# Attention's queries and row maxima laid out by DMA instead of by matrix products, its visits moved in the slot table, and a gap of three slots instead of four

## The reference, cut to what matters

```python
x = x + attn_a(layernorm(x))   # 32 heads of 4, two decaying recurrent states per head
x = x + ffn(layernorm(x))      # 8 experts of width 512, every token through all of them
x = x + attn_b(layernorm(x))   # causal softmax attention, 16 heads of 8, one shared key and value
x = x + ffn(layernorm(x))      # the same FFN weights again
```

```python
q = (x @ Wq + bq).reshape(B, T, 16, 8); k = (x @ Wk + bk)[:, :, None, :]; v = (x @ Wv + bv)[:, :, None, :]
q = rope(q); k = rope(k)
att = einsum('bthd,bThd->bhtT', q, k) / sqrt(8)
att = softmax(where(causal, -inf, att))
out = einsum('bhtT,bThd->bthd', att, v).reshape(B, T, 128) @ Wo + bo
```

## Time and profile before

| | us |
|---|---|
| runs of the kernel before | 1619.76, 1625.97, 1626.56 (median 1625.97) |
| the profiled execution | 1626.03 |
| its span | 1624.0 |
| PE busy | 1496.0 (92%) |
| DVE, ACT, POOL busy | 1177.7, 885.3, 784.3 |
| FFN tiles 9 to 13, from first gate to next first gate | 101.2 each |
| FFN tile 14 | 91.0 |
| FFN tile 15, with no attention beside it | 74.6 |
| granted clock | 1.00 from 855.0 on, but for the last us |

### The profile page before, as it was taken

The page is one execution under the profiler, slowest core; times in us unless marked ns, Lnnn a source line. Parts: engine busy times, 40 slices in busy tenths (PEclk is TensorE's granted clock), DMA queues, the critical chain, the costliest instruction groups (busy, mean ns, idle before and its releaser), DMA issues. The chain is left out here.

```text
span 1624.0 us, 23328 instructions
## 1 busy us (share of the span) xinstructions
PE 1496.0 (92%) x7504; PEld 1111.4 (68%) x7504; DVE 1177.7 (73%) x1949; ACT 885.3 (55%) x1520; POOL 784.3 (48%) x732
## 2 busy tenths in 40 slices
PE   3478999899989899899999999999999999999998
PEld 2356777677776677577567676776767767677786
DVE  5678787869778787868677585775857758577565
ACT  2245556464554546444655557565575655755554
POOL 2537445543525244531315546555465554655565
PEclk8689999999999999999999999999999999999999
DMA  6125543434334343433332334333343333433352
GB/s 202 59 71 179 198 154 119 156 117 156 140 133 156 117 156 117 156 117 117 117 133 101 118 117 150 123 131 117 119 156 121 125 117 122 156 119 124 148 182 112
DMA packets 36380, 216.28 MB, mean 133 GB/s; under 512 B 3491, under 2 KB 17444, under 8 KB 19876
## 3 DMA queue, kind: packets, MB, share of 16 engines
q1 hardware_dynamic: 36260, 214.79, 36.5%
HBM read 200.10 MB, written 15.27 MB: 133 GB/s over the span
## 5 line engine op out<-in xcount | busy, mean ns | idle before, releaser
L531 POOL TENSOR_TENSOR HL<-HF,HH 128x512 fp32r<-128x512 f32 x312 | 416.0, 1333 | 476.4 <-ACT HH L705 475.3
L1215 DVE TENSOR_TENSOR HF<-SG,bank 128x512 f32<-128x512 f32 x512 | 350.4, 684 | 171.8 <-PE bank L874 92.1
L872 PE MATMUL bank<-XTH,W 128*128 128x512 f32 x1024 | 423.4, 413 | 10.4 <-ACT SG L698 9.9
L874 PE MATMUL bank<-XTH,W 128*128 128x512 f32 x1024 | 403.8, 394 | 0.0
L873 PE MATMUL bank<-XTL,W 128*128 128x512 f32 x1024 | 403.6, 394 | 0.0
L1198 DVE SCALAR_TENSOR_TENSOR SG<-SG,bank 128x512 f32<-128x512 f32 x288 | 197.3, 685 | 207.0 <-ACT SG L700 205.0
L700 ACT ACTIVATE SG<-bank 128x512 f32<-128x512 f32 x288 | 172.1, 597 | 318.0 <-PE bank L874 316.5
L705 ACT ACTIVATE HH<-HF 128x512 fp32r<-128x512 f32 x512 | 320.4, 626 | 37.6 <-DVE HF L1215 32.4
L698 ACT ACTIVATE SG<-bank 128x512 f32<-128x512 f32 x224 | 133.5, 596 | 251.7 <-PE bank L874 250.4
L872 PEld LDWEIGHTS bank<-XTH,W 128*128 128x128 f32 x1024 | 194.4, 190 | 82.3 <-issue 23.6
L872 PE MATMUL dbank<-HH,W 128*128 128x512 f32 x512 | 217.9, 426 | 16.1 <-DVE HL L1204 14.9
(11 more groups left out here) (212 smaller groups left out, 1796.7 us busy)
## 6 DMA issues: line engine op xcount, KB each, us to landing
W<-kept_w SPq DMA_DIRECT2D x120, 1536.0 KB, 6.3
kept_w<-W SPq DMA_DIRECT2D x8, 1536.0 KB, 6.2
X<-in_L_attn_a_x_dram SPq DMA_DIRECT2D x8, 256.0 KB, 5.7
WS<-in_L_ffn_Wg_dram SPq DMA_DIRECT2D x8, 256.0 KB, 6.4
WS<-in_L_ffn_Wu_dram SPq DMA_DIRECT2D x8, 256.0 KB, 6.7
WS<-in_L_ffn_Wd_dram SPq DMA_DIRECT2D x8, 256.0 KB, 6.5
out_dram<-X SPq DMA_DIRECT2D x8, 256.0 KB, 7.2
CST<-in_tables_dram SPq DMA_DIRECT2D x1, 834.0 KB, 6.4
```

The source lines that it names most:

```text
L531: g.tensor_tensor(HL[:, n % HRING, :], HF[:, n % HFRING, :], HH[:, n % HRING, :].bitcast(F32), ALU.subtract).then_inc(F.hl, 1)
L872: pe.matmul(dst, wh, xh, start=start, stop=False)
L874: return pe.matmul(dst, wl, xh, start=False, stop=stop)
L1215: v.tensor_tensor(HF[:, n % HFRING, :], gated, fbank[(2 * n + 1) % 3], ALU.mult).then_inc(F.mul, 1)
```

## The change

Six things change together.

1. The queries' layout QST is made by DMA. SP writes QKH and QKL to DRAM (`kept_q`) and reads them back into QST, twelve reads of 8 partitions x 4 x 512 per tile. `query_stack` and its four cells are gone, with ACT's four copies. SP waits for the low part QKL and writes it before it issues the reads of the high part.
2. The maxima are transposed once per sequence (cell `mx`, `turn_maxima`, 64 columns), copied by ACT to MT, written to DRAM (`kept_m`) and read back into two free rows of each group of QST. Q2, NMP, SELR and the four `stack` cells are gone. `cols` reads QST directly, with 26 rows, and `rows` with 24.
3. The `cols` cells stand in neighbouring slots, all at point 2. PT holds six pieces in a ring instead of four, and the exponential stands ahead of ACT's gate activation instead of behind it.
4. `GAP` is 3 instead of 4, `B_LEAD` 35 instead of 36. For tile 0 the start stays the same slot.
5. The input's `turn` moves from relative slot -19 to -17, the projections from -8 to -11, and what ends the tile is one slot earlier (`fturn` 32 instead of 33).
6. SP walks the slots too, so its list now has the attention's DMAs between the weight loads.

```diff
-GAP = 4
+GAP = 3
-B_LEAD = 36
+B_LEAD = 35
-B_CELL = {"turn": (-19, 1, 3), "q": (-8, 2, 0), "qs": (-7, 1, 1), "k": (-7, 2, 2), "ks": (-6, 1, 0), "v": (-5, 1, 1),
-          "qst0": (-3, 2, 0), "qst1": (-2, 1, 1), "qst2": (-2, 2, 2), "qst3": (-1, 1, 0),
...
+B_CELL = {"turn": (-17, 1, 3), "q": (-11, 2, 0), "qs": (-10, 1, 1), "k": (-10, 2, 2), "ks": (-9, 1, 0),
+          "v": (-8, 1, 1), ("mx", 0): (8, 1, 3), ("mx", 1): (14, 1, 3), ("pv", 0, 0): (17, 1, 3),
...
-COLS_AT = [[(12, 2), (14, 0), (15, 2), (17, 0)], [(18, 2), (20, 0), (21, 2), (23, 0)]]
+COLS_AT = [[(12, 2), (13, 2), (14, 2), (15, 2)], [(17, 2), (18, 2), (19, 2), (20, 2)]]
+PT_RING = 6
...
+            def spread_queries(t, part, src, done):
+                for g in range(NG):
+                    to = RG * g + DB * part
+                    rows = kept_q[src, RG * g:RG * (g + 1), :].rearrange("(j x) t -> x j t", j=NJ)
+                    sp.dma_start(QST[to:to + DB, :, :].bitcast(F32), rows).then_inc(done, 16)
+
+            def spread_maxima(n, b):
+                sp.wait_ge(B.mt_out, 32 * (n + 1))
+                rows = kept_m[b].rearrange("(r g j) t -> g r j t", r=2, g=NG)
+                for g in range(NG):
+                    to = RG * g + 3 * DB
+                    sp.dma_start(QST[to:to + 2, :, b * SEQ:(b + 1) * SEQ].bitcast(F32),
+                                 rows[g]).then_inc(B.mrow, 16)
+
+            def side_b(t, r):
+                if r == -8:
+                    sp.wait_ge(B.hi, 2 * t + 1)
+                    after(sp, B.st_hi, 8 * 16 * t)
+                    sp.dma_start(kept_q[0], QKH[:, 0, :].bitcast(F32)).then_inc(B.hi_out, 16)
+                if r == -7:
+                    sp.wait_ge(B.lo, 2 * t + 1)
+                    after(sp, B.st_lo, 4 * 16 * t)
+                    sp.dma_start(kept_q[1], QKL[:, 0, :].bitcast(F32)).then_inc(B.lo_out, 16)
+                    sp.wait_ge(B.hi_out, 16 * (t + 1))
+                    after(sp, B.t_ready, 8 * t)
+                    spread_queries(t, 0, 0, B.st_hi)
+                    spread_queries(t, 1, 0, B.st_hi)
+                if r == -6:
+                    sp.wait_ge(B.lo_out, 16 * (t + 1))
+                    spread_queries(t, 2, 1, B.st_lo)
+                for b in range(SPT):
+                    n = SPT * t + b
+                    if r == B_CELL["mx", b][0]:
+                        sp.wait_ge(B.mt, n + 1)
...
+                            sp.dma_start(kept_m[b, :, a * P:(a + 1) * P],
+                                         MT[32 * a:32 * (a + 1), b, :].bitcast(F32)).then_inc(B.mt_out, 16)
+                    if r == B_CELL["mx", b][0] + 1:
+                        spread_maxima(n, b)
+
+            for slot in range(0, G_LAST + 1):
+                for t, r in b_tiles(slot):
+                    side_b(t, r)
+                for x in range(NE, 2 * NT * NE):
+                    u = FC * (x - WRING + 1) - 1
+                    if slot == ffn_slot(u // UNIT) + u % UNIT + LAG + 1:
+                        load_weights(x)
...
-                if n is not None:
-                    gate_act(n)
                 for t, r in b_tiles(slot):
                     for b in range(SPT):
                         for i, (at, point) in enumerate(COLS_AT[b]):
-                            if r == at + (point == 2):
+                            if r == at + 1:
                                 exps(SPT * t + b, i)
+                if n is not None:
+                    gate_act(n)
...
-            def stack2(n, b, h, bk):
-
-                pe.wait_ge(B.nml, 2 * (n + 1))
-                for x in range(2):
-                    j = 2 * h + x
-                    dst = bk[:, x * SEQ:(x + 1) * SEQ]
-                    pe.matmul(dst, SELR[:, SID, :], QST[:, j, b * SEQ:(b + 1) * SEQ], start=True, stop=False)
-                    for a in range(2):
-                        m = pe.matmul(dst[:, a * P:(a + 1) * P], NMP[:, b, a, j, :], SELR[:, SID, :],
-                                      start=False, stop=(a == 1))
-                m.then_inc(B.q2_ready, 1)
+            def turn_maxima(n, b, bk):
+
+                pe.wait_ge(B.nml, n + 1)
+                pe.transpose(bk[0:64, 0:P], NMS[:, b, :].bitcast(F32), ident).then_inc(B.mx, 1)
```

More of the change, by code:

```diff
@@ L334, in program @@
         KST = take("KST", TOK, dt=F32R)
[L335 to L339, removed]
+        assert at["now"] <= r_at
+        PT = take("PT", 3 * PT_RING, TOK)
         OS = take("OS", 2, TOK)
@@ L355, in program @@
                       "rs ay y xb z zsum zg zb done")
[L356 to L357 removed]
+        B = sems("b", "proj roped u_q u_k hi lo v_ready v_used hi_out lo_out st_hi st_lo kst_used row_ready row_used nmh nml "
+                      "mx mt mt_out mrow t_ready t_used t_cut pv os turn ro o ot otc out biased done")
         F = sems("f", "gate up sil half mul hh hl hlv down ys back done")
@@ L497, in _, with load_weights @@
             sp.dma_start(BRAW[:, C:], row(b_bk)).then_inc(ld.wb, 16)
-            for x in range(NE, 2 * NT * NE):
+            def load_weights(x):
                 sp.wait_ge(F.down, FC * (x - WRING + 1))
@@ new lines, in spread_maxima @@
+            def spread_maxima(n, b):
[25 more added lines that the diff above has]
+                        sp.wait_ge(B.mt, n + 1)
+                        after(sp, B.mrow, 4 * 16 * (n - 1))
+                        for a in range(2):
+                            sp.dma_start(kept_m[b, :, a * P:(a + 1) * P],
+                                         MT[32 * a:32 * (a + 1), b, :].bitcast(F32)).then_inc(B.mt_out, 16)
+                    if r == B_CELL["mx", b][0] + 1:
+                        spread_maxima(n, b)
@@ new lines, in _ @@
+            for slot in range(0, G_LAST + 1):
[5 more added lines that the diff above has]
+                        load_weights(x)
+                        if x % NE == 4 and x // NE > NT:
+                            t = x // NE - NT - 1
+                            sp.wait_ge(F.done, NT + t + 1)
+                            sp.dma_start(o_tok[:, t], X[:, t, :, :]).then_inc(stored, 16)
@@ L775, in exps @@
             def exps(n, i):
+                m = (4 * n + i) % PT_RING
                 act.wait_ge(B.t_ready, 4 * n + i + 1)
-                after(act, B.pv, 2 * n)
-                act.activation(PT[:, 3 * i:3 * i + 3, :], three, ACT.Exp, scale=DB ** -0.5).then_inc(B.t_used, 1)
+                after(act, B.pv, 2 * (n - 1) if i < 2 else 2 * n)
+                act.activation(PT[:, 3 * m:3 * m + 3, :], three, ACT.Exp, scale=DB ** -0.5).then_inc(B.t_used, 1)
             def side_b(t, r):
@@ L810, in side_b @@
                             act.activation(OS[:, z, :], abank, ACT.Copy).then_inc(B.os, 1)
-                    for h in range(2):
-                        if r == B_CELL["stack", b, h][0]:
-                            act.wait_ge(B.q2_ready, 2 * n + h + 1)
-                            after(act, B.t_ready, 4 * (n - 1))
-                            act.activation(Q2[:, b, 2 * h:2 * h + 2, :], r3(sbank[bank_of(("b", t, ("stack", b, h)))], 2),
-                                           ACT.Copy).then_inc(B.q2_used, 1)
+                    if r == B_CELL["mx", b][0]:
+                        act.wait_ge(B.mx, n + 1)
+                        after(act, B.mt_out, 32 * (n - 1))
+                        act.activation(MT[0:64, b, :], sbank[bank_of(("b", t, ("mx", b)))][0:64, 0:P],
+                                       ACT.Copy).then_inc(B.mt, 1)
                     if r == B_CELL["ot", b][0]:
@@ L840, in _ @@
                 n = unit_of(slot)
-                if n is not None:
-                    gate_act(n)
+                if slot == b_slot(0):
+                    act.wait_ge(A.done, NT)
+                    act.wait_ge(A.z, NT)
                 for t, r in b_tiles(slot):
@@ L1482, in _ @@
                 n = unit_of(slot)
+                if slot == b_slot(0):
+                    v.wait_ge(A.z, NT)
+                    v.wait_ge(A.done, NT)
                 new_maxima(slot, 2)
```

153 lines of the change are left out of this document (58 added, 95 removed), and 2 rows, old and new, of the table B_CELL.

## The result

The changed kernel takes **1674.06 us** (median of 3 runs, 1673.77 to 1674.5), the kernel before 1625.97. The ratio is 1.031, 95% interval 1.027 to 1.035: slower by 48 us, where 1614 and a range of 1589 to 1634 were forecast.

The account below looks back on a forecast made before the run. PE, busy 92% of the span, was taken as the bound. FFN tiles 8 to 13 -1.5 us, tile 7 -4.4, tile 14 -1.9, tile 6 -1.1, gap -3: together -11.9 from 1626.0, so 1614, range 1589 to 1634.

Parts of the forecast that it names:

- lands at 7.8 + 6.3 = 14.1: Slot 23's weight load, issued 7.8 us into it, lands 6.3 later; PE waits 2.7 us at slot 28.
- the reads pile up: Rival, 0.08: twelve reads at half a weight load's rate delay the load behind by 1 us in six tiles; 1620.
- SyncE's issues: Behind the wait for QKL, thirteen DMAs at 0.47 us each, 6.1 us, precede slot 23's weight load.
- issues are slow: Rival, 0.09: SP takes 0.85 us a read issue, not 0.47; wait at slot 28 is 7.6 us; 1649.
- The clock: After PE's pause at slot 28, half clock for 3.4 us loses 1.7; half counted, 0.85 us a tile.
- PE's savings and the small terms: Each full tile: PE saves 4.8 us net; ACT costs 0.3, layer norm 0.2, the wait for maxima 0.5.
- the change doesn't pack: Rival, 0.03: cols products of 24 and 26 rows run one behind another, 0.26 us a cell; 1647.
- the maxima's reads: Second sequence's reads land 9.35 us into slot 12, its first cols cell due at 9.1; wait counted 0.5 us.
- The exponential first: Exponential ahead of the gate activation fits cols slots except slot 10, behind four XN activations: 0.3 us a tile lost.
- The gap: Between unit 255's and unit 256's gates, one slot fewer lets XTL end sooner: 3 us saved, between 0 and 5.
- Tiles 6 and 7: FFN tile 6: -1.9 plus a 0.8 us weight wait, -1.1; tile 7: no weight wait, -4.4.
- no weight wait: Rival, 0.27: the load lands within slot 28's start, so neither wait nor clock loss in six tiles; 1592.

Follow-up runs that it names:

- e4: Changed kernel with the edits of e1 and e2 together; 1598.63 us, ratio 0.986 to the kernel before.
- e7: e4 with ScalarE's gate activation put back ahead of the exponential; 1617.61 us, ratio 0.996 to the kernel before.
- e9: e8 with a slot's weight load issued ahead of the attention transfers of that slot; 1602.81 us, ratio 0.985 to the kernel before.
- e6: e5 with a slot's weight load issued ahead of the attention transfers of that slot; 1634.23 us, ratio 1.007 to the kernel before.
- e8: e5 with each of its three copies to DRAM written by 4 transfers of 32 partitions instead of one transfer; 1634.10 us, ratio 1.008.
- e2: Changed kernel with a slot's weight load ahead of its attention transfers, and the low part's write and first 8 reads one slot later; 1650.12 us, ratio 1.017.
- e1: Changed kernel with each query read writing every third partition of 24 instead of 8 neighbouring ones; 1643.04 us, ratio 1.013 to the kernel before.
- e10: Changed kernel with a tile's first 8 reads writing every second partition, the last 4 neighbours; scores not the reference's; 1647.9 us in one run.
- e3: Changed kernel with the 8 reads of the high part issued ahead of the low part's write; 1655.63 us, ratio 1.020 to the kernel before.
- e5: Changed kernel with three copies of the queries written to DRAM and 4 reads of 24 partitions instead of 12 of 8; 1664.83 us, ratio 1.025.

## Why the prediction was wrong, point by point

**The step that failed** is the landing of the weight load, "lands at 7.8 + 6.3 = 14.1". The place, the wait and its readers were right: gate of slot 28, FFN tiles 8 to 13, the load of slot 23 behind the queries' transfers. The 6.3 was read from loads that found the queue empty. Behind twelve slow reads it was 14.2 to 16.6, so PE waited 9.8 to 11.2 us and not 2.7 (7.7 and not 0.8 ahead of tile 7), and these seven waits are 70.1 us where six of 2.7 and one of 0.8 are 17. The rival "the reads pile up" had the mechanism, with a chance of 0.08 and a price of 1 us a tile. It took half the rate of a weight load for the reads, which from 1536 KB in 6.3 us is 125 GB/s, and they run at 59. At that rate their 768 KB take 13.3 us. 4.1 of these are over when the load is issued, and 9.2 + 6.3 = 15.5 is what was measured. The number of engines was weighed there and the partitions they write were not; it is the second that does the harm.

**SyncE's issues.** 0.34 us and not 0.47, so the load is issued 1.6 us earlier than forecast. The rival "issues are slow" would have given the right sign by the wrong cause, and the sign that the prediction set for it, a wait over 5 us, came without it.

**The clock.** Forecast 0.85 us for each wait. The tile of 111.19 us less e4's 97.58 is 13.6, and the wait is 11.15 of it. Some 2.4 us are left, which PE lost at 0.50 after the pause. That is the most of the six tiles: they are 72.5 us longer than e4's, 62.4 of it are the waits, and the other 10 make 1.7 us a tile. The forecast had taken half of that.

**PE's savings and the small terms.** Their sum was right. Without the wait the forecast for a full tile is 101.2 - 4.8 + 0.3 + 0.2 + 0.5 = 97.4, and e4's is 97.58. The turn in slot 12 has no wait any more, the maxima's transposition lasts 0.27 us but delays what follows by less, and cols products of 26 rows take what 32 did:

```profile
1099.54 0.51 PE L1051 MATMUL three<-QST,KST 26*128 26x512 f32 x3 [0.88 <-ACT PT L812]
...
1101.59 0.27 PE L1093 MATMUL abank<-CST,NMS 128*64 128x128 f32 x1
1101.62 0.47 PE L901 MATMUL dbank<-HH,W 128*128 128x512 f32 x1
1101.93 0.39 PE L902 MATMUL dbank<-HL,W 128*128 128x512 f32 x1
...
1104.41 0.60 PE L938 MATMUL abank<-CST,XN 128*128 128x128 f32 x4
1104.77 0.47 PE L901 MATMUL dbank<-HH,W 128*128 128x512 f32 x1
...
1105.63 0.50 PE L1051 MATMUL three<-QST,KST 26*128 26x512 f32 x3
1106.06 0.50 PE L901 MATMUL bank<-XTH,W 128*128 128x512 f32 x1
```

They answer to the earlier trace rows: the turn takes 0.36 to the next start (0.38), the cols cell 0.43 (0.43). Around the transposition the two starts are 0.03 and 0.31 us apart where 0.23 each is usual, so it costs PE about 0.1 us and not 0.15 to 0.2. So "the change doesn't pack" is out. No row shows PE waiting for the maxima's reads, for which 0.5 us was counted. The one wait behind the four XN activations, counted at 0.3, is 0.88 here and 5.7 us in seven places, and makes up for it. That the sum comes out to 0.2 us is in part luck. Tile 14 lost 1.7 us in the changed kernel (91.0 to 89.3), 1.9 forecast.

**The exponential first** was counted as a small loss of 0.3 us a tile. e7 shows that without it 17 to 19 us would be lost. The sum came out right since the saving of it was nowhere counted: the forecast took for granted that cols cells in neighbouring slots don't wait.

**The gap** was forecast at -3 and is longer in the changed kernel, 12.7 us against 11.5. One microsecond of it is a new wait for the queries' reads, and PE's clock there is 0.95 on average. Even in e4, which has neither, it is 11.1. The waits of e4 in that stretch:

```profile
PE abank L952 <- ACT XNF L737: 1.8, 1, 1.8
PE three L1030 <- DVE NM L1379: 1.0, 1, 1.0
```

XTL is no longer last, as forecast: it starts 9.6 us after unit 255's gate and not 10.5. PE waited for the norm ahead of the turn and for the first maxima before too, for 0.9 and 1.1 us; with one slot less it waits 1.8 and 1.0. Behind these waits PE has its own products until unit 256's gate, and doesn't wait for XTL. The step took DVE's queue for the only limit.

**Tiles 6 and 7.** Forecast -1.1 and -4.4. Without the gap tile 7 is 102.6 us before and 100.3 in e4, -2.2; where the other 2.2 went isn't traced. Tile 6 is 97.0 before, 99.7 in the changed kernel with its wait of 7.7, and 93.9 in e4 although 3.1 of waiting is left. Tile 5, where nothing was expected, is 94.8 us in e4 and 91.9 before. Its last stretch, in e4 and then before:

```profile
633.50:640.00 6.50, 5.97 (x16) 4.89 (x17) 3.40 (x6) 3.94 (x8) 0.00 (x0) 0.50 0.00 0
```
```profile
631.50:637.60 6.10, 4.18 (x20) 3.25 (x21) 3.12 (x6) 5.85 (x13) 0.66 (x2) 1.00 0.01 4
```

PE waits as long in both (8.0 and 8.2 us in the tile), and in e4 it then runs at 0.50 for 6 us, which loses the 2.9. e7, which has all of e4's edits, has tile 5 at 92.0. So it is clock, and no edit's work; why the clock fell in one and not in the other stays open.

**With the reads out of the way** e4's 1598.6 stands 6.6 above the 1592 that the rival "no weight wait" gave. The gap accounts for 2.6 of it and tile 7 for 2.2; tile 5's 2.9 less 1.1 gained in tile 6 is the rest.

PE's wait for weights or queries in the profiled execution and the median time go together over these kernels, if not in every step:

| kernel | PE waits for weights or queries, us | time, us |
|---|---|---|
| e4 / e9 | 3.1 / 3.3 | 1598.6 / 1602.8 |
| e6 | 28.9 | 1634.2 |
| e8 | 30.7 | 1634.1 |
| e2 | 33.8 | 1650.1 |
| e1 | 35.6 | 1643.0 |
| e10 | 44.1 | 1647.9 |
| e3 | 50.0 | 1655.6 |
| e5 | 55.0 | 1664.8 |
| changed | 71.1 | 1674.1 |

From e4 to the changed kernel it is 75.4 us of time for 68.0 of waiting. Clock lost after the pauses is more than the rest, 10 us in tiles 8 to 13; tiles 0 to 5 are 5.6 us shorter in the changed kernel and hide part of it.

## What to carry to other kernels

A transfer moved onto a queue costs whatever stands behind it there, so read how long its packets will hold the queue, not only how long it takes to issue. For that look at both ends: the slowest dimension of either side, which sets the engines, and how the written partitions are spread, which sets how fast each packet goes. Put the load that PE needs next ahead of bookkeeping transfers, and then look at who reads those.

## What the hardware showed that was not expected

- Reads into 8 neighbouring partitions run at 59 GB/s together and hold a load behind them for 8 to 10 us more. In steps of three a packet takes 102 ns and not 281, and queued reads move 145 GB/s.
- SyncE issues such a read every 0.34 us, and one whose partitions have a step of two or three every 0.70 (7.14 us for 8 stepped and 4 plain in e10).
- A write whose DRAM side has a slowest dimension of 4 runs on 4 engines: 6.2 us and not 2.0 for 256 KB.
